# A decoder layer's feed-forward block: the raw gate's fetches move from SyncE's DMA queue to ScalarE's

## The reference, cut to what matters

```python
x = act_qdq(x)
up = act_qdq(x @ lpbq_dequant(w_up).T)
gate = act_qdq(x @ lpbq_dequant(w_gate).T)
sig = fixed_qdq_u16(jax.nn.sigmoid(gate))
gate = act_qdq(gate * sig)
o = act_qdq(gate * up)
return o @ lpbq_dequant(w_down).T
```

## Time and profile before

| what | us |
|---|---|
| median of 3 runs | 1980.45 (1980.31 to 1984.59) |
| the profiled execution's own time | 1984.42 |
| its span, first to last instruction | 1982.7 |
| TensorE busy | 1850.0 (93%) |
| VectorE busy | 1577.7 (80%) |
| ScalarE busy | 1198.9 (60%) |
| GpSimd busy | 433.3 (22%) |

### The profile page before, as it was taken

One profiled execution on the slowest core, in us unless ns is written; L12 is line 12 of the kernel. 1 busy time (PEld: TensorE's weight loads), 2 busy tenths in 40 slices (PEclk: granted clock), 3 DMA queues, 4 the chain that ended last, 5 costly groups with the idle time before them and its releaser, 6 DMA issues. The chain is left out here.

```text
span 1982.7 us, 70407 instructions
## 1 busy us (share of the span) xinstructions
PE 1850.0 (93%) x28023; PEld 1309.8 (66%) x28023; DVE 1577.7 (80%) x2891; ACT 1198.9 (60%) x2016; POOL 433.3 (22%) x531
## 2 busy tenths in 40 slices
PE   7999999999999977999999999999599999799798
PEld 4677766676766666888888888887344443244687
DVE  6777777777767774888888888888499877688897
ACT  4455445444544434777777777776355677788565
POOL 1112211211111121233333332323111133100121
PEclk9999999999999978999999999999799999899899
DMA  5111111111111012121212121210188799598584
GB/s 148 37 35 36 44 42 35 39 40 41 35 37 46 26 32 72 45 65 42 63 43 62 44 62 44 61 45 22 22 262 269 272 350 354 204 414 373 197 270 147
DMA packets 169445, 221.91 MB, mean 112 GB/s; under 512 B 80691, under 2 KB 142390, under 8 KB 169270
## 3 DMA queue, kind: packets, MB, share of 16 engines
q1 hardware_dynamic: 169270, 219.22, 33.5%
HBM read 116.40 MB, written 94.37 MB: 106 GB/s over the span
## 5 line engine op out<-in xcount | busy, mean ns | idle before, releaser
L1540 PE MATMUL ff_twin<-ff_xq,w_uh 128*128 (+1 forms) x1152 | 346.0, 382 | 29.1 <-ACT ff_whole L1694 12.6
L1540 PEld LDWEIGHTS ff_twin<-ff_xq,w_uh 128*128 128x128 f16 x1152 | 112.3, 98 | 171.1 <-issue 26.4
L1540 PE MATMUL ff_twin<-ff_xq,w_ul 128*128 (+1 forms) x576 | 219.8, 382 | 0.0
L721 DVE TENSOR_TENSOR x<-rec_x,rec_until 128x512 f32<-128x512 f32 x256 | 158.9, 682 | 49.9 <-PE rec_x L401 49.9
L573 ACT ACTIVATE x<-rec_e,rec_hidden 128x512 f32<-128x512 f32 x256 | 158.1, 688 | 54.6 <-PE rec_e L418 54.6
L307 POOL TENSOR_TENSOR rec_o<-rec_tmp 128x512 f32<-128x512 f32 x32 | 68.2, 2132 | 560.4 <-DVE rec_tmp L771 560.4
L1266 DVE TENSOR_REDUCE mneg<-att_s 128x4 f32<-128x512 f32 x256 | 158.8, 682 | 26.7 <-PE att_s L1037 26.7
L541 ACT ACTIVATE rec_v<-rec_f 128x256 f32<-128x256 f32 x64 | 24.5, 383 | 206.3 <-DVE rec_z L730 206.3
L430 PE MATMUL rec_x<-x 32*32 32x64 f32 x8192 | 141.1, 219 | 8.1 <-issue 7.7
L430 PEld LDWEIGHTS rec_x<-x 32*32 32x32 f32 x8192 | 123.4, 107 | 35.0 <-issue 34.7
L748 DVE TENSOR_TENSOR rec_tmp<-rec_x,x 128x512 f32<-128x512 f32 x128 | 79.7, 682 | 83.9 <-POOL rec_o L309 70.0
(11 more groups left out here) (253 smaller groups left out, 4486.3 us busy)
## 6 DMA issues: line engine op xcount, KB each, us to landing
raw_scratch<-ff_out SPq DMA_DIRECT2D x32, 768.0 KB, 3.5
ff_in<-raw_scratch SPq DMA_DIRECT2D x32, 768.0 KB, 6.8
gate_scratch<-ff_out SPq DMA_DIRECT2D x28, 768.0 KB, 7.7
ff_in<-gate_scratch SPq DMA_DIRECT2D x28, 768.0 KB, 9.1
product_scratch<-ff_out SPq DMA_DIRECT2D x28, 768.0 KB, 8.7
ff_out<-product_scratch SPq DMA_DIRECT2D x28, 768.0 KB, 6.1
turned_scratch<-rec_xT SPq DMA_DIRECT2D x32, 256.0 KB, 2.9
att_x<-in_x SPq DMA_DIRECT2D x32, 256.0 KB, 2.8
```

What stands on the lines that cost most here:

```text
L721: V.tensor_tensor(mt[:, b].rearrange("p (a j m) n -> p j a m n", a=KC, m=2)[:, j], X[j].rearrange("p (a m n) -> p a m n", a=KC, m=2), unti ...
L1540: m = T.matmul(bank_.rearrange("p (b n) -> p b n", b=BT), weights(wp, kc, a, c), tile[:, xp, :, kc], start=(i == 0), stop=(i == len(terms) ...
```

## The change

Three things are done. SyncE's stream loses `refill` and keeps, in sweep 2, the 28 stores alone. ScalarE gets a `refill` of its own, called in `gate` between `rounds` and `sigmoid` of the same half; it waits for the same semaphore value, and for the tile's raw values to have reached memory, which SyncE used to wait for once ahead of all. The DMA is issued by ScalarE into its own queue. And the loop over ScalarE's tiles is written out (16 steps in place of 8 rounds of 2). The number of fetches, which tile each brings, the buffers and the arithmetic are as before.

```diff
-                def refill(m, n, s):
-                    sp.wait_ge(q["rounded"], m * FC + (s + 1) * HC)
-                    fetch_raw(n, s)
-
...
-                refill(0, 3, 0)
                 for m in range(NT - 2):
-                    u = m % 2
-                    refill(m, (m + 3) % NT, 1)
-                    store(g_d, m, m + 2, u, 0)
-                    refill(m + 1, (m + 4) % NT, 0)
-                    store(g_d, m, m + 2, u, 1)
-                refill(NT - 2, 1, 1)
+                    for s in range(2):
+                        store(g_d, m, m + 2, m % 2, s)
...
+                def refill(m, n, s):
+
+                    act.wait_ge(q["rounded"], m * FC + (s + 1) * HC)
+                    act.wait_ge(raw_out[n % 2][s], 16 * (2 + n // 2))
+                    A.dma_start(src[:, s], part(r_d, n, s)).then_inc(raw_in[s], 16)
+
                 def gate(m, u, before):
                     for s in range(2):
                         act.wait_ge(raw_in[s], 16 * (m + 1))
                         rounds(m, u, s, 1, lambda c, k: src[:, s, k * TOK:(k + 1) * TOK])
+                        if m < NT - 1:
+                            refill(m, (m + 3) % NT, s)
                         sigmoid(m, u, s, before)
...
-                with act.Fori(0, NT // 2) as j:
-                    for u in range(2):
-                        gate(2 * j + u, u, j)
+                for m in range(NT):
+                    gate(m, m % 2, m // 2)
```

## The result

The changed kernel takes 1990.71 us (median of 19 runs, 1983.44 to 1997.73), the kernel before 1986.51 in as many runs on the same chips (1980.31 to 1997.36): a ratio of 1.0026, 95% interval 1.0014 to 1.0038. That is some 5 us slower, where 10.8 us faster were forecast, and outside the range. The forecast stood on a median of three runs, 1980.45; over 19 runs the kernel before takes 6 us more than that, so of the 21.1 us between the forecast of 1969.6 and 1990.71, 6.1 are its starting point. The profiled execution has a span of 1988.0 us.

The account below looks back on a forecast made before the run. The prediction took sweep 2's fetch-rounding-fetch loop as the bound: steps falling from 8.78 to 8.1 us over 16 steps save 10.8 us, from 1980.45 to 1969.6 us. The range was 1963.5 to 1981.5.

Parts of the forecast that it names:

- What bounds it now: Sweep 2: the loop fetch, rounding, next fetch sets the 8.96 us step; DMA share 0.98 does not show engines at their limit.
- A queue of their own: Sweep 2's fetches in a separate queue take 4.2 to 6.1 us, taken as 6.0, for a step of 8.1 us.
- The upper end: Bound on a sweep 2 fetch sharing packet for packet with a store: 6.1 us, a step of 8.2.
- It can't stand behind another fetch: Sweep 2's two halves are issued about 4 us apart, so one fetch's data part is over before the other's.
- The turns: Each DMA engine alternates between the queues' rings a packet at a time, so a fetch beside stores moves at half rate.
- SyncE without the fetches: Start of sweep 2: fetches no longer stand behind a store's wait; 1.9 of ScalarE's 2.63 us idle go.
- The issue on ScalarE: Each fetch issue adds 0.43 us to a ScalarE half in sweep 2, costing nothing until fetches are faster than 5.7 us.
- The loop: Writing out ScalarE's sweep 2 loop removes register instructions from an idling engine: 0, at most 0.1 us per step.
- The DMA engines are the bound: Rival for sweep 2: 355 GB/s at most whatever the queue, step 8.9 us, about 1980 us; no change, chance 0.13.
- ScalarE's issue is dear: Rival for sweep 2: an issue holding ScalarE 1.15 us makes a step 9.4, total 1988 us; slower, chance 0.12.
- The floors: Least sweep 2 step from DMA data 7.6, ScalarE 7.76, TensorE 7.77 us; reaching 7.8 gives 1964.8 us, chance 0.10.
- A: Theory from the follow-up experiments: a fetch finding its queue empty costs each DMA engine extra time, about 0.6 us, at first packets.

Follow-up runs that it names:

- the second small-DMA run: Kernel before, loop written out, fetches on SyncE; ScalarE issues 30 DMAs of 16 x 64 bytes, each to its own place, without waiting for landings: 0.9995.
- the first small-DMA run: Kernel before, loop written out, fetches on SyncE; ScalarE issues 30 DMAs of 16 x 64 bytes, each waiting for the one before to land: 1.0063.

## Why the prediction was wrong

- *Where it started.* 6.1 of the 21.1 us between forecast and result are the median of three runs that it was counted from. The other 15.0 are the 10.8 that did not come and the 4.2 that were lost.
- *What bounds it now.* The loop fetch, rounding, fetch was read rightly. The step that failed began here: I set the DMA share of 0.98 aside, since it "counts a packet that waits as much as one that moves". It does, but the packet times of all queues together come to at most 1.03 of the 16 engines in any stretch of 80 us looked at here: an engine has about one packet at a time, and one that waits holds it. The engines were nearly full, at 8.7 of a step's 8.8 us, and sharing them otherwise among queues could free little. They can move 404 GB/s in this mix, so the loss was in the waiting packets, and the change did not touch it.
- *A queue of their own.* This term was mis-sized. I bounded a fetch by 4.2 us alone and 6.1 when shared, and took 6.0; it took 6.9. The upper end was no bound. It let a fetch share with one store whose data cost 1.90 us of engine time, the price of sweep 3. Its own slow start was in the 4.2 already (a fetch without any store beside takes 4.3 and costs 49.6 us a megabyte); that of the other fetch was not. Fetches cost 51.3 us a megabyte in place of 38.4, which is 1.573 x 12.9 / 16 = 1.3 us more of every engine per step; the kernel before lost 3.15 x 5.6 / 16 = 1.1 us in the same way. So the separate queue removed none of it. The 2.5 us that a fetch stood behind others in the one queue were not time to be had back: with three buffers in one queue fetches take longer, 8 us to landing, and the sweep is shorter.
- *"It can't stand behind another fetch."* Also not so: they are issued 3.9 to 7.1 us apart and take 6.9, so two are mostly under way at once. How the 0.8 us above the bound divide between this and the slow start, no run separates. The turns themselves were taken rightly: from 1609.0 to 1609.3 us the engines started 12 packets of ScalarE's queue and 10 of SyncE's.
- *SyncE without the fetches.* Right in kind: the wait of 2.63 us at the start is gone. The sum left out that the first four issues on ScalarE are hidden by no wait and take 1.8 of it; 0.8 came back.
- *The issue on ScalarE.* Right: 0.43 was forecast, 0.5 measured, hidden by the wait, as the second small-DMA run shows (0.9995).
- *The loop.* Right, nothing.
- *Rivals.* "The DMA engines are the bound" was the nearest, with 355 GB/s and no change; 339 came. Its reason, a rate for this mix, was wrong: 404 GB/s go through with a half more lead. So was its course: the stores landed sooner, not the fetches. The rule quoted beside it from the Trainium skill, "DMA: Bandwidth & Descriptors", section "Issuing engines are not separate DMA queues", held as to the gain, for none came. "ScalarE's issue is dear" did not happen; the kernel came out slower all the same, and the cause of that is open.
- *The floors* at 7.6 to 7.8 us were real: with earlier fetches the sweep falls to 121 to 127 us, 7.6 to 8.0 per step, and TensorE has no gap between 1600 and 1680.

A is shown in what it says of time: the price is there with no store beside, with all reads from one tile, in all three queues tried, and most of it goes when the fetch is issued earlier. That explains why nothing was gained. It does not explain the 0.26% that were lost: the engine time of a step, 8.9 us in place of 8.7, differs by less than two profiles of like kernels do. What is also open is A's trigger. In the changed kernel many fetches were issued while the one before had not landed, so "empty queue" is too narrow; whether an emptied queue counts or a minimum time between issue and turn, no run here separates. Nor is it shown what an engine waits for in that time.

## What to carry to other kernels

Before moving transfers to another queue, multiply the DMA share by engines and time, divide by the bytes, and compare with a stretch of similar transfers at its best (here 44.0 against 38.4 us of engine time a megabyte). If they differ and the share is near 1, the engines are full of packets that wait, and another queue will not empty them. Here the loss came of late issue. Issue fetches earlier, if need be in pieces as each piece of the buffer comes free; that brought here what the second queue was to bring. An experiment that adds an instruction must not add a wait with it: the first small-DMA run would have "shown" a wrong theory at 1.0063. And a forecast of half a per cent should not start from a median of three runs.

## What the runs showed of the hardware

- Fetches of 768 KB in a queue of their own cost the DMA engines 49.6 to 51.3 us per megabyte when issued two halves ahead (50.4 from GpSimd) and 41.5 when issued three ahead; the stores in the queue beside cost 38.5 to 39.5. In one queue with the stores the mean was 42.5 to 45.4 against 39.9.
- The one read looked at closely, alone on the engines and issued late, started its packets 0.9 us after its issue and moved 63 to 251 GB/s for about 1 us.
- The packet times of all queues came to at most 1.03 of 16 engines in any stretch of 80 us or more that was looked at.
- Packets of 2 KB in place of 6 KB, in one queue with the stores, took 41.2 us a megabyte, less than the late 6 KB ones.
- A DMA of 16 x 64 bytes took 5.0 us (median) to land beside the large ones, when issued into an otherwise unused queue.
- An issue took 0.33 us (median) on ScalarE, 0.33 to 0.43 on SyncE, and 0.58 on GpSimd.
